# Another order of the work, on all five engines, in a fused gated cross-attention and quantised feed-forward kernel

## The reference

```python
# x (16, 256, 512), ctx (16, 256, 128), float32; 16 heads of 32; I = 1408
x = x + tanh(g_xattn) * xattn(layernorm(x), ctx)
x = x + tanh(g_ffn) * ffn(layernorm(x))

def xattn(q, latent, Wq, Wkv, Wout):          # causal, 16 heads
    qp = q @ Wq.T
    k, v = split(latent @ Wkv.T, 2, axis=-1)
    attn = softmax(where(causal, qh @ kh.T / sqrt(32), min))
    return (attn @ vh) @ Wout.T

def ffn(x, w_gate_up, w_down):                # dq(): round to a row's max/127 and back
    gate, up = split(dq(x) @ dq(w_gate_up).T, 2)
    return dq(silu(gate) * up) @ dq(w_down).T
```

## Time and profile before

| | us |
|---|---|
| median of 3 runs | 755.83 |
| lowest, highest | 751.87, 756.05 |
| the profiled execution, its own time | 755.35 |
| span of its instructions | 753.4 |
| opening, to the first pair of slot 1 | 84.82 |
| slots 1 to 13 and the start of the ending | 84.82 to about 463.7 |
| a slot in the middle, by the starts of its first pair | 29.16 |
| feed-forward tiles 6 to 31 | about 548 to 753.4 |

### The profile page before, as it was taken

One profiled execution on the slowest core, in us unless ns is written; L12 is line 12 of the kernel. 1 busy time (PEld: TensorE's weight loads), 2 busy tenths in 40 slices (PEclk: granted clock), 3 DMA queues, 4 the chain that ended last, 5 costly groups with the idle time before them and its releaser, 6 DMA issues.

```text
span 753.4 us, 16996 instructions
## 1 busy us (share of the span) xinstructions
PE 709.7 (94%) x5321; PEld 512.0 (68%) x5345; DVE 624.6 (83%) x1900; ACT 413.4 (55%) x658; POOL 575.1 (76%) x763
## 2 busy tenths in 40 slices
PE   4599799999999999999999999988999999999994
PEld 4578578878888888888888786655544444444441
DVE  3687587888978978878879868789999999999994
ACT  5447467577576576585674663464544443434431
POOL 4458587797797797887887965668888888888884
PEclk9689999999999999999999999999999999999998
DMA  9797686977967978868869649992746655656657
GB/s 247 207 240 198 147 221 167 227 182 192 257 169 203 224 189 223 196 191 212 214 186 222 162 126 217 260 202 55 151 124 149 159 132 144 155 130 149 145 126 203
DMA packets 137982, 137.57 MB, mean 183 GB/s; under 512 B 90381, under 2 KB 99879, under 8 KB 137767
## 3 DMA queue, kind: packets, MB, share of 16 engines
q1 hardware_dynamic: 136832, 135.97, 72.7%
q10 hardware_dynamic: 1063, 0.54, 0.4%
HBM read 40.24 MB, written 25.31 MB: 87 GB/s over the span
## 4 chain that ended last, share of the span: by engine, by line
PE 78%; DVE 7%; DMA 5%; issue 4%; SPq 3%; POOL 2%; ACT 1%; ACTq 0%; DVEq 0%; POOLq 0%
PE psum L2020 17%; PE psum L1639 11%; PE psum L1661 10%; PE psum L1703 9%; PE psum L2030 7%; PE psum L1592 5%; PE psum L1677 4%; PE psum L1590 4%; PE psum L1626 3%; PE psum L1649 3%; DVE hmax L1500 2%; PE psum L1576 2%; PE psum L1679 2%; SPq L374 2%; DMA xln<-x_dram 1%
## 5 line engine op out<-in xcount | busy, mean ns | idle before, releaser
L1229 DVE CUSTOM_DVE_ANT_0 junk<-psum,mask 128x128 f32<-128x128 f32 (+1 forms) x512 | 153.6, 353 | 64.2 <-PE psum L1592 62.1
L2020 PE MATMUL psum<-w1q,xqb 128*128 128x512 bf16 (+1 forms) x755 | 156.9, 361 | 3.7 <-DVE u L1270 1.4
L926 ACT ACTIVATE prob<-psum 128x768 f32<-128x768 f32 x128 | 103.6, 810 | 51.3 <-PE psum L1679 49.8
L800 POOL TENSOR_TENSOR hidden<-hidden 128x512 f32<-128x512 f32 (+1 forms) x94 | 110.5, 1191 | 27.7 <-ACT hidden L1144 27.4
L2020 PEld LDWEIGHTS psum<-w1q,xqb 128*128 128x128 bf16 x768 | 74.3, 98 | 82.1 <-DVE u L1270 1.6
L1149 ACT ACTIVATE hidden<-hidden,round_bias,hinv 128x1408 f32<-128x1408 f32 x31 | 48.4, 1561 | 107.7 <-DVE hinv L1510 107.7
L615 POOL TENSOR_SCALAR_AFFINE_SELECT prob<-prob 128x512 f32<-128x512 f32 x128 | 82.4, 647 | 29.2 <-ACT prob L926 28.0
L623 POOL TENSOR_TENSOR prob<-prob 128x256 f32<-128x256 f32 x128 | 97.8, 770 | 6.2
L2030 PE MATMUL psum<-w2q,hqT 128*128 128x512 bf16 x330 | 78.1, 385 | 6.1 <-DMA hqT<-hq 5.5
L1639 PE MATMUL psum<-xT_hi,wq_hi 128*128 128x256 f32 x256 | 75.0, 293 | 3.9 <-POOL xT_lo L630 3.0
L1592 PE MATMUL psum<-heads 96*128 96x256 f32 x256 | 76.3, 334 | 0.0
(11 more groups left out here) (125 smaller groups left out, 1807.9 us busy)
## 6 DMA issues: line engine op xcount, KB each, us to landing
heads<-k_hi SPq DMA_DIRECT2D x128, 128.0 KB, 4.4
heads<-q_hi SPq DMA_DIRECT2D x128, 128.0 KB, 4.2
xln<-x_dram SPq DMA_DIRECT2D x16, 512.0 KB, 5.4
heads<-k_lo SPq DMA_DIRECT2D x64, 128.0 KB, 3.9
heads<-q_lo SPq DMA_DIRECT2D x64, 128.0 KB, 4.0
x<-x_dram SPq DMA_DIRECT2D x16, 512.0 KB, 4.3
x_scratch<-x SPq DMA_DIRECT2D x16, 512.0 KB, 4.1
x1b<-x_scratch SPq DMA_DIRECT2D x32, 256.0 KB, 3.4
```

The source lines that it names most:

```text
L800: pool.tensor_tensor(up[t % 3][:, o], gate[t % 3][:, o], up[t % 3][:, o], ALU.mult).then_inc(f["prod_done"], 1)
L926: act.activation(prob[:, g % 2, pair % 2, 0:CAUSAL // P].rearrange("p k h q -> p h k q"), psum[:, 2:4, 0:CAUSAL].rearrange("p h (k q) -> p ...
L1229: dve.tensor_tensor_reduce(junk[:, n % 2, 0:w], psum[:, h % 2, cols], m, 1.0, LOWEST, ALU.add, ALU.max, mx[:, X % 2, t, h:h + 1]).then_inc ...
L2020: last = pe.matmul(psum[:, bank, 0:w], xqb[:, t % 4, k, :], w1q[:, k, half * I + o:half * I + o + w], start=(k == 0), stop=(k == KH - 1))
```

## The change

Every list of calls is written in another order; the computation and its sizes are the same. In the slot, on TensorE, each `weigh` stands further behind the pairs that feed it, the four `output` halves stand in the middle instead of the end, the first `scores` come earlier, and one `values` step is moved to the end of the slot before (so the opening has one more `values` and the ending one less). `WORK` is changed to match. `residual`, `measure` and `rsqrt2` of a batch are all in one slot, and the quantisation of a piece of the weights comes one slot later. SyncE issues the last quarter-spreads of k at the start of the next slot. In the opening, the first piece of w2 is loaded behind the rows of batch 1, VectorE's 3.5 us fill of ones stands at its very start (the other one at the opening's end), `high_q` of batch 0 stands before `norm1` of batch 1, and there are 15 products of 512 columns whose result nobody reads (`spare`). In the ending, SyncE's list and the weaving with tiles 0 to 5 are new.

```diff
-        WORK = [("V", 0, 1, 7), ("V", 1, 1, 6), ("Q", 1, 2, 7), ("K", 0, 2, 6), ("K", 1, 2, 7), ("T", 0, 3, 6),
-                ("O", 0, -1, 6), ("T", 1, 3, 7), ("O", 1, -1, 7), ("Q", 0, 3, 6)]
+        WORK = [("V", 1, 1, 6), ("Q", 1, 2, 6), ("K", 0, 2, 7), ("K", 1, 2, 6), ("O", 0, -1, 7), ("T", 0, 3, 6),
+                ("T", 1, 3, 6), ("O", 1, -1, 6), ("Q", 0, 3, 7), ("V", 0, 2, 6)]
...
-                load_piece(0)
...
-                    if is_piece(i) and i > 0:
-                        sp.wait_ge(s["w_int"], i)
+                    if is_piece(i):
+                        wait_for(sp, s["w_int"], i)
                         load_piece(i)
...
                 def slot(b):
+                    spread_k_lo(b + 1, 2)
+                    spread_k_lo(b + 1, 3)
+                    store_x1(b - 2)
+                    spread_k_hi(b + 1, 3)
+                    move_weights(b + 1)
+                    load_residual(b - 1)
+                    load_context(b + 3)
+                    spread_q_hi(b + 2, 0)
+                    spread_q_lo(b + 2, 0)
+                    spread_q_lo(b + 2, 1)
+                    spread_k_hi(b + 2, 0)
+                    spread_k_lo(b + 2, 0)
                     store_xq(b - 3)
-                    load_context(b + 3)
-                    load_weights(b + 3)
-                    move_weights(b + 2)
-                    load_residual(b - 1)
-                    spread_q_hi(b + 2, 0)
+                    spread_q_lo(b + 2, 2)
                     spread_q_hi(b + 2, 1)
+                    load_rows(b + 4)
+                    spread_k_lo(b + 2, 1)
                     spread_q_hi(b + 2, 2)
                     spread_q_hi(b + 2, 3)
-                    spread_q_lo(b + 2, 0)
-                    spread_q_lo(b + 2, 1)
-                    spread_q_lo(b + 2, 2)
+                    spread_k_hi(b + 2, 1)
                     spread_q_lo(b + 2, 3)
-                    load_rows(b + 4)
-                    spread_k_hi(b + 2, 0)
-                    spread_k_hi(b + 2, 1)
                     spread_k_hi(b + 2, 2)
-                    spread_k_hi(b + 2, 3)
-                    spread_k_lo(b + 2, 0)
-                    spread_k_lo(b + 2, 1)
-                    spread_k_lo(b + 2, 2)
-                    spread_k_lo(b + 2, 3)
-                    store_x1(b - 1)
+                    load_weights(b + 3)
 
                 def ending():
+                    spread_k_lo(B - 1, 2)
+                    spread_k_lo(B - 1, 3)
+                    store_x1(B - 4)
+                    spread_k_hi(B - 1, 3)
                     load_w1()
+                    load_residual(B - 3)
+                    store_xq(B - 5)
...
                 def opening():
+                    ones(0)
                     measure_x(0)
                     low_weights(0, wkv_hi, wkv_lo, wkv_raw)
                     low_weights(1, wq_hi, wq_lo, wq_raw)
-                    weigh_rows(0)
                     measure_x(1)
-                    ones(1)
                     split_q(0, 0)
                     split_q(0, 1)
-                    ones(0)
-                    weigh_rows(1)
-                    for h in range(0, 4):
+                    spread_rows()
+                    weigh_rows(0)
+                    for h in range(0, 6):
                         maxima(0, h)
...
                 def slot(b):
-                    measure(b - 2, 1)
-                    split_q(b + 2, 0)
                     normalise(b - 1, 0)
                     normalise(b - 1, 1)
                     measure_x(b + 3)
-                    low_o(b - 1, 0)
                     maxima(b + 1, 0)
                     maxima(b + 1, 1)
+                    split_q(b + 2, 0)
+                    maxima(b + 1, 2)
+                    maxima(b + 1, 3)
+                    low_o(b - 1, 0)
+                    maxima(b + 1, 4)
+                    maxima(b + 1, 5)
                     split_q(b + 2, 1)
-                    for h in range(2, 6):
-                        maxima(b + 1, h)
-                    low_o(b - 1, 1)
-                    for h in range(6, 13):
+                    for h in range(6, 10):
                         maxima(b + 1, h)
                     step(b - 2, 0)
-                    for h in range(13, 16):
-                        maxima(b + 1, h)
+                    maxima(b + 1, 10)
+                    maxima(b + 1, 11)
+                    low_o(b - 1, 1)
+                    maxima(b + 1, 12)
+                    maxima(b + 1, 13)
+                    step(b - 2, 1)
+                    maxima(b + 1, 14)
+                    maxima(b + 1, 15)
                     negate(b + 1)
-                    step(b - 2, 1)
-                    weigh_rows(b + 3)
-                    if b + 3 == PIECES - 1:
+                    weigh_rows(b + 2)
+                    if b + 2 == PIECES - 1:
                         dve.tensor_scalar(w_scale[:, W1T:NW], w_scale[:, W1T:NW], gates[:, 1:2], None,
                                           ALU.mult).then_inc(s["gate_step"], 1)
                     residual(b - 1, 0)
+                    residual(b - 1, 1)
...
+                def spare(bank, n):
+
+                    if bank == 4:
+                        pe.wait_ge(s["v_copied"], 2)
+                    for i in range(n):
+                        pe.matmul(psum[:, bank, :], wkv_hi[:, 0:P], wkv_hi[:, 0:H], start=True, stop=True)
+
                 def opening():
                     transposed(0, 0)
+                    pe.wait_ge(s["t_copied"], 1)
                     transposed(0, 1)
+                    values(0, 0)
                     keys(0, 0)
                     keys(0, 1)
-                    values(0, 0)
                     values(0, 1)
-                    pe.wait_ge(s["t_copied"], 1)
                     queries(0, 0)
                     queries(0, 1)
                     pe.wait_ge(s["t_copied"], 2)
                     queries(0, 2)
                     queries(0, 3)
-                    pe.wait_ge(s["q_lo"], 1)
+                    spare(0, 3)
+                    pe.wait_ge(s["q_lo"], 2)
                     transposed(1, 0)
-                    pe.wait_ge(s["q_lo"], 2)
+                    spare(0, 3)
+                    pe.wait_ge(s["t_copied"], 3)
                     transposed(1, 1)
-                    pe.wait_ge(s["t_copied"], 3)
-                    queries(1, 0)
+                    spare(0, 9)
                     scores(0, 0)
                     scores(0, 1)
-                    queries(1, 1)
+                    pe.wait_ge(s["q_lo"], 1)
+                    queries(1, 0)
                     scores(0, 2)
                     scores(0, 3)
+                    queries(1, 1)
+                    scores(0, 4)
+                    scores(0, 5)
...
                 def slot(b):
                     score_pair(b, 0)
+                    values(b + 1, 1)
                     broadcast(b - 1, 0)
                     broadcast(b - 1, 1)
-                    values(b + 1, 0)
                     score_pair(b, 1)
-                    values(b + 1, 1)
                     queries(b + 2, 2)
-                    score_pair(b, 2)
-                    queries(b + 2, 3)
-                    score_pair(b, 3)
                     scores(b + 1, 0)
                     scores(b + 1, 1)
-                    weigh(b, 0)
+                    queries(b + 2, 3)
                     scores(b + 1, 2)
                     scores(b + 1, 3)
-                    score_pair(b, 4)
+                    score_pair(b, 2)
                     keys(b + 2, 0)
                     scores(b + 1, 4)
                     scores(b + 1, 5)
-                    keys(b + 2, 1)
-                    score_pair(b, 5)
+                    score_pair(b, 3)
+                    weigh(b, 0)
                     scores(b + 1, 6)
                     scores(b + 1, 7)
-                    weigh(b, 1)
+                    score_pair(b, 4)
+                    keys(b + 2, 1)
                     scores(b + 1, 8)
-                    score_pair(b, 6)
                     scores(b + 1, 9)
+                    output(b - 1, 0, 0)
                     scores(b + 1, 10)
                     transposed(b + 3, 0)
-                    score_pair(b, 7)
                     scores(b + 1, 11)
+                    score_pair(b, 5)
+                    weigh(b, 1)
                     scores(b + 1, 12)
-                    weigh(b, 2)
                     scores(b + 1, 13)
-                    scores(b + 1, 14)
-                    output(b - 1, 0, 0)
-                    scores(b + 1, 15)
+                    score_pair(b, 6)
                     transposed(b + 3, 1)
                     output(b - 1, 0, 1)
+                    scores(b + 1, 14)
+                    scores(b + 1, 15)
+                    score_pair(b, 7)
+                    output(b - 1, 1, 0)
                     maxima_rows(b + 1)
+                    output(b - 1, 1, 1)
+                    weigh(b, 2)
```

(5 more changed lines are left out.)

672 lines of the change are left out of this document (333 added, 339 removed).

## The result

The changed kernel takes **744.51 us** (median of 4 runs, 739.03 to 745.93) beside 755.17 for the kernel before on the same chip: a ratio of 0.9847, 95% interval 0.9806 to 0.9887, 10.7 us. A second series gave 742.76 and 0.9836 (0.9808 to 0.9864). The profiled execution took 743.81 with a span of 742.0, 11.5 us under that of before. The sum said 741.35.

A forecast was written before the change was run, and what follows sets the result against it. The prediction took TensorE, busy 94% of the span, as the bound, with time to win only where it stands or runs at the lower clock. 755.35 - 5.2 (slots) - 6.5 (opening) - 2.3 (ending) = 741.35 us, range 731 to 753.

The forecast's parts named there:

- Slots: Slots 1 to 13: 0.4 us of TensorE's waits gained in each, 5.2 us in all; bounds 7.8 gained, 13 lost.
- the 0.6 of the earlier trace: One slot's TensorE waits for row maxima, 0.6 us in 3 pieces; taken as the most to win, 7.8 over 13 slots.
- Two heads cost 0.46 wherever they stand: Slots: a couple of heads' scores takes 0.46 us in any place, so nothing was counted for moving them.
- Opening: Up to slot 1's first pair: 6.5 us gained, a little over half of at most 11.2; bounds 0 and 11.
- The 4 us of the transposes: Opening: batch 1's transposes start at about 24.7 instead of 28.66, 4 us earlier, with q_lo done at about 24.3.
- The 2.9 of the clock: Opening: spare products keep TensorE's clock up from 33.62 to 39.50, 2.9 us gained, their own cost taken as nothing.
- The 2.6 of the moved maxima: Opening's end: slot 1's first pair waits 2.58 us for the moved row maxima, which may go wholly or partly.
- The rival of the spreads: Opening: spreads hold it, so it gains only 1 us; total 746.9, chance 0.10.
- Ending: Ending: 2.3 us gained from VectorE's wait for x, one values step and shorter waits; bounds 1 lost, 5 gained.
- VectorE as the bound of the first scores: Slots: VectorE's 0.60 us a head holds the earlier scores, so slots gain nothing; total 746.6, chance 0.14.
- The late spreads of k: Slots: k's last spreads, issued 2.1 us into the next slot, make each wait 1.1; total 760.9, chance 0.07.
- Waits only moved: Slots and ending: reordering only moves waits, gain 2 to 4 us, near 752; chance 0.13, shared with both single rivals together.

The follow-up runs named there:

- experiment 7: Kernel before, with TensorE's scores of heads 0 to 7 each one step earlier in the slot: 754.56 us, ratio 1.0011, period 29.17.
- experiments 5 to 8: Kernel before with heads 8 to 13 coupled (758.18 us), further apart (754.84), or as in experiment 7; changed kernel with heads 10 and 11 coupled (743.64).
- experiment 10: Kernel before, with VectorE's second fill of ones ahead of batch 1's norm and ScalarE's two q_hi ahead of that norm: 756.28 us, ratio 1.0023.
- experiment 1: Changed kernel without the 15 spare products of its opening: 742.70 us, ratio 0.9843.
- experiment 9: Changed kernel with w2's second row block load and first block's store put behind the first half of batch 1's spreads: 756.11 us, ratio 1.0021.

## Why the prediction was right, and where it was not

The forecast was 741.35 and the changed kernel took 743.81 in the profiled execution, but of its three terms one was too small by 3 us and two too large by 3 and 2. That the sum came within 2.5 us is in part luck.

**Slots: 5.2 said, 8.2 measured** (slot 1 1.6 on the means, slots 2 to 12 6.1, slot 13 0.5; 8.7 in the one pair of profiles, where slot 1 gave 2.0). The period of 28.6 to 28.9 came as named. But the 7.8 that the prediction called the most an order can win was passed. The step that was mis-sized is the one slot taken for all. The earlier trace rows show one of 29.16 to 29.17; from the seventh on they lasted 29.2 to 29.5, with up to 0.2 lost at the border of two slots, its first pair waiting for the moved row maxima; and slot 1 lasted 30.8, 1.4 of it in its second pair's wait for exponentials that the late first pair had pushed back. The remark that the maxima have 7 us to the next pair stood in the prediction and had no price.
Nor is the 0.6 of the earlier trace rows what was won. TensorE's sixteen heads fell from 4.78 to 4.01 us a slot, counted from start to start, and the maxima's transposes from 0.31 to 0.14; the queries (+0.21), values (+0.10) and the rest (+0.17) took some back, for each change of kind of step moved to another border. The sum is 0.47 in this slot, its period's difference (29.17 - 28.70). Of the three rows of 0.2 two lie behind a `weigh`, where the new order has the same distance (the next load starts 0.98 after the start of the last row of loads, 239.69 to 240.67 and 233.38 to 234.36), and were no loss; the third, in front of head 10, is. That leaves 0.2 to 0.3 for the wait and 0.15 to 0.25 for borders, by the rows; experiment 7 shows 0.1 of the second part by itself, and no experiment brought the old slot down to 28.70.
"Two heads cost 0.46 wherever they stand" was misread. The old slot has 0.60 for a couple that a `weigh` follows and 0.56 for one behind a `weigh`; 0.46 is the least, in the earlier trace rows as in the new slot, where heads 8 and 9 start at 236.11 and end their part at 236.58, and experiments 5 to 8 got no couple under it. So the borders that the prediction left at nothing were worth up to half of a slot's gain. The Trainium skill's N / 2.4 + 2.5 ns (TensorE: Matmul & The Clock Gate, Back-to-back issue gap) is given there for a product by itself, and the section adds that it falls short for small products that come each with their own load; the 0.33 that it makes for a couple is in no profile here. The 27 us that the prediction drew from it also count 16 couples a slot, where sixteen heads make eight: 13.5 us.

**Opening: 6.5 said, 3.2 measured on the means** to slot 1's start (3.3 in the pair of profiles). "Slot 1 at 78 or so" was missed in it (81.5), by less than the 82 set as the limit, and met by one of the others (78.4). The named transposes came at 25.55, before 26, and the clock stayed at 1.00 from there to 45:

```profile
25.55 0.63 PE L1579 MATMUL psum<-ident,xln 128*128 128x128 f32 x4 [0.78 <-DVE q_lo L1259]
...
37.44 1.09 ACT L895 ACTIVATE q_hi<-psum 128x512 fp32r<-128x512 f32 x2 [6.85 <-DMA heads<-q_lo]
...
52.67 0.30 PE L1593 MATMUL psum<-heads 96*128 96x128 f32 x1 [1.87 <-DMA heads<-k_lo]
```

Three steps of the term failed. The 4 us of the transposes were measured against 28.66, the latest of four profiles of the old opening (25.4 to 28.7, mean 26.7); the gain on the means is 1.3. The old ones start 6.75 after the rows have landed, 2.5 of it for the fill and q_hi (experiment 10); in the new order the rows are there at 17.7 and it is q_lo, done at 25.4 and not at 24.3, that the transposes wait for. The 2.9 of the clock were kept where they were named and bought nothing: ScalarE stood 6.85 for the spread of q of batch 0, and the clock fell again from 45 to 59 (0.78, 0.74), so that with the spare products gone slot 1 came no later than in the unedited profiles (experiment 1). Nor were they free: they put the first scores of batch 0 off by 1.6. The 1.7 of the second low stretch stayed: TensorE is busy for all of the 6.55 us at 0.74, which is 1.7 again. The 2.6 of the moved maxima was got whole: no profile of the new order has that wait, all of the old have 2.6 to 3.6. With slot 1's shorter length it is the larger part of the 4.7, by the rows; no experiment took it alone. The rival of the spreads, at one in ten, was nearer to the opening than the forecast; but its mechanism is shown only in part, by ScalarE's 6.85 and by TensorE's 1.87 at 52.67, which three of the five new openings don't have, and experiment 9 found the first scores of batch 1 no earlier with fewer transfers ahead of the spreads.

**Ending: 2.3 said, 0.5 measured in the pair of profiles and nothing that shows on the means.** The residual's wait for x (4.28) is gone, as named, and TensorE's 1.01 behind it. In its place stands a wait that no rival had: the maxima of batch 15 behind the steps' load, which the reordered queue had brought ahead of them: 1.67 and then 5 us at 0.66 of the clock, another 1.7. From the ending's first product to the last `down` ahead of the closing's tile it is 268.5 before and 268.05 after, 0.5 less. The sign named for it, tile 6 at 83 us or less after the ending's start, against 84.3 in the kernel before, asked for 1.3 less; the `down` inside tile 6 starts 90.5 after the ending's start before and 89.9 now, 0.7 less, so this sign did not come.

**The rivals.** VectorE as the bound of the first scores did not show: no score of the new slot waits for a maximum. The late spreads of k did not either: issued at 226.49, 1.4 into the slot (2.1 had been reckoned), they were in before ScalarE's k_hi at 233.96, which had no wait for them. "Waits only moved" is the ending's story alone.

## What to carry over

Read the stretch between steps' starts in every slot, not one, and take more than one profile of an opening: its start moved by 3 us with no line changed, and a term set against the latest one is too large. Ask what a late step's start keeps a fixed distance to from one profile to the next: here the landing of one load. A wait of a couple of tenths in an ordered list belongs to a run of steps that is too dense; moving one of them hands it to the next, and only distance over the whole run takes it away. Before a small, urgent transfer ask which large one has been issued in the microsecond around it, and before a clock is bought with spare products whether that stretch waits for TensorE at all.
